# A recommendation tower on one core: first table looked up by high and low parts, TensorE run beforehand on the identity, and another order of units, turns and grams for the first tiles

## The reference

```python
e = stack([tbl_f[ids[:, f]] for f in range(26)], axis=1)       # 2048 x 26 x 128
combined = concatenate([e, r_dense_x[:, None, :]], axis=1)     # 2048 x 27 x 128
z = einsum('bfd,bgd->bfg', combined, combined)[:, triu_i, triu_j]
h = concatenate([z, r_dense_x], axis=1)                        # 2048 x 479
h = maximum(h @ W_top1 + b_top1, 0)                            # 512
h = maximum(h @ W_top2 + b_top2, 0)                            # 256
y = h @ W_top3
```

## Time and profile before

| | us |
|---|---|
| median of 3 runs | 369.84 |
| the three runs | 369.84, 367.74, 370.93 |
| profiled execution, first to last instruction | 368.7 |

### The profile page before, as it was taken

The page is one execution under the profiler, slowest core; times in us unless marked ns, Lnnn a source line. Parts: engine busy times, 40 slices in busy tenths (PEclk is TensorE's granted clock), DMA queues, the critical chain, the costliest instruction groups (busy, mean ns, idle before and its releaser), DMA issues.

```text
span 368.7 us, 12553 instructions
## 1 busy us (share of the span) xinstructions
PE 339.9 (92%) x5616; PEld 282.4 (77%) x5616; DVE 170.0 (46%) x388; ACT 187.5 (51%) x260; POOL 259.5 (70%) x265
## 2 busy tenths in 40 slices
PE   1999889698999999999999999999999999889677
PEld 0488877586888888887888788888888888877576
DVE  3599955555254635356255535356255534202020
ACT  2399831553636734583627634483627633564313
POOL 6788877777777777777777777777777777776000
PEclk9999999999999999999999999999999999999989
DMA  6969394244243333423242334424232222222000
GB/s 231 338 198 245 95 281 129 54 114 94 58 118 80 81 94 100 103 71 112 66 110 80 89 87 100 106 70 110 65 111 80 66 52 73 54 53 72 3 4 1
DMA packets 19369, 37.33 MB, mean 101 GB/s; under 512 B 5525, under 2 KB 8213, under 8 KB 19316
## 3 DMA queue, kind: packets, MB, share of 16 engines
q1 hardware_dynamic: 11124, 19.74, 18.6%
q0 software_dynamic: 8192, 16.79, 17.4%
HBM read 36.51 MB, written 0.01 MB: 99 GB/s over the span
## 4 chain that ended last, share of the span: by engine, by line
POOL 57%; issue 20%; PE 13%; DVE 5%; DMA 3%; ACT 2%; POOLq 0%; SPq 0%
POOL rows L263 57%; DVE onehot L298 3%; PE ps_lk L552 3%; PE ps_lk L576 2%; PE ps_gram L602 2%; DMA h<-in_tbl 2%; PE ps_lk L657 2%; DVE table L304 1%; DMA rows<-in_tbl,gather_ids 1%; PE ps_lk L672 1%; PE ps_mlp L636 1%; PE ps_zt L629 1%; ACT xt L374 0%; PE ps_zt L636 0%; PE ps_mlp L629 0%
## 5 line engine op out<-in xcount | busy, mean ns | idle before, releaser
L263 POOL DMA_INDIRECT rows<-in_tbl,gather_ids x256 | 258.2, 1009 | 79.7 <-issue 77.1
L298 DVE TENSOR_SCALAR onehot<-ids 128x512 fp32r<-128x512 f32 (+1 forms) x328 | 126.8, 442 | 84.0 <-PE ps_lk L576 51.2
L576 PE MATMUL ps_lk<-onehot,table 128*128 128x512 f32 (+1 forms) x704 | 155.3, 374 | 4.5 <-DVE onehot L298 3.4
L576 PEld LDWEIGHTS ps_lk<-onehot,table 128*128 128x128 f32 x704 | 120.5, 190 | 25.7 <-issue 5.3
L384 ACT COPY xt<-ps_tr 128x512 f32<-128x512 f32 x64 | 76.8, 1200 | 73.9 <-PE ps_tr L587 73.9
L312 DVE STREAM_TRANSPOSE zs<-ps_gram 128x832 f32<-128x832 f32 x16 | 16.8, 1050 | 99.9 <-PE ps_gram L602 99.9
L602 PEld LDWEIGHTS ps_gram<-xt 128*26 128x26 f32 x4096 | 44.0, 104 | 23.3 <-issue 20.3
L602 PE MATMUL ps_gram<-xt 128*26 128x26 f32 x4096 | 53.0, 193 | 9.2 <-issue 4.8
L371 ACT COPY xt<-ps_lk 128x512 f32<-128x512 f32 x35 | 42.0, 1235 | 21.6 <-issue 9.6
L587 PE MATMUL ps_tr<-ident,rows 128*128 128x128 f32 x256 | 39.4, 276 | 2.6 <-DMA rows<-in_tbl,gather_ids 2.3
L587 PEld LDWEIGHTS ps_tr<-ident,rows 128*128 128x128 f32 x256 | 29.9, 140 | 9.5 <-issue 4.0
(11 more groups left out here) (59 smaller groups left out, 157.6 us busy)
## 6 DMA issues: line engine op xcount, KB each, us to landing
ids<-in_ids_onehot SPq DMA_DIRECT2D x41, 256.0 KB
rows<-in_tbl,gather_ids POOLq DMA_INDIRECT x256
w<-in_tbl SPq DMA_DIRECT2D x6, 512.0 KB, 6.7
zt<-in_tbl SPq DMA_DIRECT2D x3, 512.0 KB, 7.0
dense_x<-in_dense SPq DMA_DIRECT2D x8, 128.0 KB
zt<-in_dense SPq DMA_DIRECT2D x8, 128.0 KB, 2.7
h<-in_tbl SPq DMA_DIRECT2D x1, 512.0 KB, 6.1
w<-in_w SPq DMA_DIRECT2D x1, 512.0 KB
```

The costliest lines, as they stand in the source:

```text
L263: pool.indirect_dma_start(rows[n % ROW_BUFS][:, r, :], None, t_[f"tbl_{GATHERED[r]}"], bass.IndirectOffsetOnAxis(ap=gather_ids[:, n, r:r + ...
L298: nc.vector.tensor_scalar(onehot[:, k, 0:w], ids[e % IDS][:, 0:w].bitcast(F32), float(k), None, ALU.is_equal).then_inc(s_unit, 1)
L576: m = nc.tensor.matmul(ps_lk[e % LB][:, x], table[:, i, part, k, :], onehot[:, k, x], start=(k == 0 and j == 0 and part == 0), stop=(k == ...
```

## The change

Five things change.

1. Step 0 is looked up like the others, from the high and low parts. Table 0 is split first, in two halves of four k each (`FIRST_PARTS`), ScalarE and VectorE each with two operations of half the size. `lookup(0)` waits for each half. `split_count(j)` is the number of splitting operations after which table j is ready, since table 0 now counts two.
2. Staging: all five buffers are used in turn by all ten tables.
3. TensorE multiplies the identity with itself 20 times into an unused PSUM bank ahead of the first lookup (`WARM_UP`).
4. VectorE makes the units of the fourth step of chunk 1 ahead of pack(1), and in the middle of the units of step 0 the two halves of table 0 are subtracted. ScalarE's order of rounding, shifting ids and copying is altered to suit in the first steps.
5. TensorE's turns, lookups and grams of tiles 0 to 2 are in another order.

```diff
-SPLIT = list(range(1, NO)) + [0]
+FIRST_PARTS = 2
+WARM_UP = 20
...
-        RAWS = len(stage) - 1
-        raw = [stage[0] if j == 0 else stage[1 + SPLIT.index(j) % RAWS] for j in range(NO)]
+        RAWS = len(stage)
+        raw = [stage[j % RAWS] for j in range(NO)]
...
+        def split_count(j):
+            return FIRST_PARTS + j
...
-                n = SPLIT.index(j)
-                if j > 0 and n >= RAWS:
-                    sp.wait_ge(s_low, n - RAWS + 1)
+                if j >= RAWS:
+                    sp.wait_ge(s_low, split_count(j - RAWS))
...
-            sp.wait_ge(s_low, NO)
+            sp.wait_ge(s_low, split_count(NO - 1))
...
+            def low_first(part):
+                k = slice(part * KT // FIRST_PARTS, (part + 1) * KT // FIRST_PARTS)
+                dve.wait_ge(s_high, part + 1)
+                nc.vector.tensor_tensor(table[:, 0, 1, k, :], raw[0][:, k, :],
+                                        table[:, 0, 0, k, :].bitcast(F32), ALU.subtract).then_inc(s_low, 1)
...
-            make_units(0)
+            make_units(0, range(0, 4))
+            low_first(0)
+            make_units(0, range(4, 6))
+            low_first(1)
+            make_units(0, range(6, KT))
             for e in range(1, STEP0[1]):
...
-            low(NO - 1)
...
+            def high_first(part):
+                k = slice(part * KT // FIRST_PARTS, (part + 1) * KT // FIRST_PARTS)
+                act.wait_ge(s_raw[0], 16)
+                nc.scalar.copy(table[:, 0, 0, k, :], raw[0][:, k, :]).then_inc(s_high, 1)
...
-            def lookup_first():
-                pe.wait_ge(s_raw[0], 16)
-                for k in range(KT):
-                    pe.wait_ge(s_unit, k + 1)
-                    m = nc.tensor.matmul(ps_lk[0][:, :], raw[0][:, k, :], onehot[:, k, :].bitcast(F32),
-                                         start=(k == 0), stop=(k == KT - 1))
-                    if k % USE == USE - 1:
-                        m.then_inc(s_unit_used, 1)
+            def warm_up():
+                for _ in range(WARM_UP):
+                    nc.tensor.matmul(ps_zt[:, 0:P], ident[:, :], ident[:, :], start=True, stop=True)
...
+                    if e == 0 and k % (KT // FIRST_PARTS) == 0:
+                        pe.wait_ge(s_low, k // (KT // FIRST_PARTS) + 1)
...
-            lookup_first()
+            warm_up()
+            lookup(0)
```

More of the change, by code:

```diff
@@ L291, in _, with make_units @@
         def _(dve):
-            def make_units(e):
-                dve.wait_ge(s_from, e + 1)
-                for k in range(KT):
+            def make_units(e, ks=range(KT)):
+                if ks[0] == 0:
+                    dve.wait_ge(s_from, e + 1)
+                for k in ks:
                     if k % USE == 0 and e > 0:
@@ L325, in _ @@
             nc.vector.tensor_copy(first[:, :], first_i[:, :]).then_inc(s_first, 1)
-            make_units(0)
+            make_units(0, range(0, 4))
[3 more added lines that the diff above has]
+            make_units(0, range(6, KT))
             for e in range(1, STEP0[1]):
-                for n in range(len(STEPS[e][2])):
-                    low(STEPS[e][2][n] - 1)
+                for j in STEPS[e][2]:
+                    low(j)
                 make_units(e)
-            low(NO - 1)
             dve.wait_ge(s_const, 3)
@@ L353, in _, with high @@
         def _(act):
-            def high(n):
-                j = SPLIT[n]
+            def high_first(part):
+                k = slice(part * KT // FIRST_PARTS, (part + 1) * KT // FIRST_PARTS)
+                act.wait_ge(s_raw[0], 16)
+                nc.scalar.copy(table[:, 0, 0, k, :], raw[0][:, k, :]).then_inc(s_high, 1)
+            def high(j):
                 act.wait_ge(s_raw[j], 16)
@@ L422, in _ @@
             shift(0)
-            high(0)
+            high_first(0)
+            high_first(1)
+            high(1)
             shift(1)
-            high(1)
+            high(2)
+            shift(2)
             evac(0)
-            shift(2)
             evac_group(0, 0)
-            high(2)
+            high(3)
             shift(3)
             evac(1)
-            high(3)
+            high(4)
             shift(4)
@@ L435, in _ @@
             evac_group(0, 1)
-            high(4)
             high(5)
@@ L443, in _ @@
             evac(4)
+            evac_group(0, 3)
             high(7)
-            evac_group(0, 3)
+            high(8)
             shift(7)
             evac(5)
-            high(8)
+            evac(6)
             high(9)
+            evac_group(1, 0)
             shift(8)
-            evac(6)
-            evac_group(1, 0)
             evac_dense(0)
@@ L699, in _ @@
             e = STEP0[1]
+            turn(1, 1)
             gram(0, 0)
-            turn(1, 1)
             lookup(e)
@@ L704, in _ @@
             gram(0, 1)
+            lookup(e + 1)
             turn(1, 3)
-            lookup(e + 1)
+            lookup(e + 2)
             gram(1, 0)
-            lookup(e + 2)
+            turn_pairs(0)
             gram(1, 1)
@@ L713, in _ @@
                 a, e, f = c * CT, STEP0[c], STEP0[c + 1]
-                turn_pairs(a - 2)
+                if c > 1:
+                    turn_pairs(a - 2)
                 if c == 1:
@@ L731, in _ @@
                     turn(a, 3)
-                gram(a, 0)
-                lookup(f)
+                    lookup(f)
+                    gram(a, 0)
+                else:
+                    gram(a, 0)
+                    lookup(f)
                 turn(a + 1, 0)
```

14 lines of the change are left out of this document (5 added, 9 removed).

## The result

The changed kernel takes 367.54 us, the median of 14 runs (364.89 to 422.55), the kernel before 370.42 in the 14 runs beside it (367.74 to 371.54). The ratio is 0.9924, with a 95% interval of 0.9899 to 0.9949: 2.8 us faster, between 1.9 and 3.7. The profiled execution of the changed kernel took 366.06 us on the device for a span of 363.6. The difference, some 2.4 in the changed kernel's runs, is 1.7 in those of the kernel before, so 0.7 us of what the spans gain is given back outside them.

The account below looks back on a forecast made before the run. The prediction took GpSimd's back-to-back gathers, the last one's landing and a fixed tail as the bound. The ninth gather's stall (0.82 us) plus less stretching (0.6) made 1.4 us off the median of 369.84: 368.4, range 365.8 to 370.9.

Parts of the forecast that it names:

- within 1%: Whole kernel: the measured time lies within 1% (3.7 us) of the time before; given 0.82.
- Term one: Ninth gather, waiting for k = 3 of the first lookup: its stall goes, 0.82 us gained.
- Term two: Gathers stretched by VectorE's subtractions: somewhat fewer caught than before, 0.6 us gained.
- TensorE is some 8 us ahead at 80 us: TensorE's early part: a lead of 3.7 us and 4 us, plus the wait at turn(1, 3).
- A distance so constant ... is a wait for the rows: Tiles 6 to 12: turn(n, 3) starts 4.01 to 4.14 us after its gather, so TensorE waits for rows to land.
- the 4.0 it must have: turn(3, 3): it must start 4.0 us after its gather; at 8.45 it had 4.4 us of room.
- What it gains early it waits away: TensorE, faster than the gathers by some 0.4 us a round, loses any early lead in waits for rows.
- A fixed tail: From turn(15, 1) to the end: the last 36.5 us are TensorE's and ScalarE's own and stay.
- Rival A: Whole kernel: TensorE is the bound, so its lead of 8.2 us survives whole, 361.6 us; 8%.
- B: First 42 us: VectorE, packed tighter, stretches gathers more, 3.1 us lost against 0.82 gained, 372.1 us; 12%.
- C: New waits at turn(3, 3) and turn(4, 3) let the clock fall, costing 1.6 us if late, 370.0 us; 10%.
- D: Lookup 0: the warm-up ends late and the clock is low, most of the ninth gather's stall stays, 369.2 us; 5%.

Follow-up runs that it names:

- experiment 1: Changed kernel with ScalarE's rounding of table 9 moved ahead of the copy of lookup 6, two sets: 367.12 us (0.9929) and 368.02 us (0.9961).
- reorder alone: Kernel before with only the new order of VectorE's units and TensorE's turns, lookups and grams: 370.68 us, ratio 1.0000.
- experiment 2: One gather fewer a tile from tile 2 on: on the changed kernel 362.39 us, on that with table 9's rounding moved 361.59, on the kernel before 366.16.
- experiment 3: Changed kernel with GpSimd's gathers held once ahead of tile 3, until four units of lookup 11 are used: 370.06 us, ratio 1.0006.
- experiment 5: Changed kernel with the warm-up removed: 369.92 us, ratio 0.9982.
- lookup alone: Changed kernel with the old order of tiles 0 to 2 on TensorE and VectorE, two sets: 372.15 us (0.9969) and 370.54 us (0.9992).

## Why the prediction was right, and where it was wrong

The number came out: 367.54 for 368.4, within the range, and "within 1%" was the case that held. But the gain was 2.8 where 1.4 was forecast, and its reason covers only a part; that the rest stayed within the range is luck, since no term had it. The account in spans: at turn(15, 3) the two changed profiles are 2.2 and 1.5 us early, the tail is 2.9 shorter, and 0.7 is lost outside the span: 4.4 and 3.6, against 2.8 and 3.5 by the two ratios.

- Term one, the stall of the ninth gather: right that it goes. But the gather starts at 14.44 for the 14.07 of the forecast, 0.45 earlier than before and not 0.82, in the first profile. The second lookup (13.32 for 13.8) and the warm-up (8.02, within 6.0 to 10.3) are near where they were put.
- Term two, less stretching: right in the sum for the first profile (1.61 by the last gather for 1.4), most of it from here: the seventeenth gather is only 0.11 earlier than before, the thirty-third 1.50. But the second profile of the same kernel has the last gather 1.74 earlier still, so single gathers stretch differently from one execution to the next, and a term of 0.6 was below what one profile can carry.
- "TensorE is some 8 us ahead at 80 us": wrong. At turn(2, 3), near 84 us, it was 0.16 behind in the first profile and 2.9 ahead in the second, at turn(3, 3) 1.2 ahead in both. The sum followed VectorE's work alone and left out ScalarE's new order, whose rounding of table 9 came 3.85 us late for VectorE; and the lookup near 70 us, which was to lose its wait and run at the upper level, took 6.78 us.
- "A distance so constant ... is a wait for the rows": the conclusion holds for the kernel before, the argument does not. Before, the last packet of the rows ended 0.41 to 0.58 us ahead of the turns of tiles 6 to 12, as at turns held by name (0.31 to 0.94 in four profiles), and these turns start 0.20 to 0.31 us behind the start of the matmul ahead of them, 0.11 in the changed kernel. So they were held, but by 0.1 to 0.2 us each, some 1.1 in all with turn(15, 1). After the change the distance is as constant, 5.17 to 5.18, with the rows there 2.98 to 3.01 us ahead.
- Such constancy is not chance either: in the eleven profiles with all gathers, 41 of the 44 distances at these tiles lie within 3.9 to 4.3, 5.1 to 5.3, 6.4 to 6.5, 7.7 to 7.8 or 8.9 to 9.0, one gather step of 1.25 apart. Something couples the two streams, mostly without a wait of either; VectorE, which waits for TensorE and stretches gathers, could, but no run isolates it. And "the 4.0 it must have" fell: turns held by name measured 2.70 to 4.22 from tile 4 on.
- "What it gains early it waits away": half right. An earlier TensorE gained nothing (experiment 1, reorder alone), but hardly more where fewer gathers could not hold it (experiment 2); later gathers cost time (experiment 3). And a later TensorE costs time as well (experiment 5, lookup alone). The streams look balanced within a microsecond or two, and that the change pays because it moves both is argued from these runs, not shown.
- "A fixed tail": wrong, and the largest error in size. The 36.5 us from turn(15, 1) became 33.4.
- Rival A (TensorE bound, 361.6) had the bound that the page after shows, but not the 8 us. B did not come: the last gather is not later. C did come, at 42 and 70 us and not at the waits for rows. D did not.

The runs sorted by their mean granted clock show no shift of the bound (means in us, with the count of runs; those of the kernel before are from the experiments):

| clock | before | changed |
|---|---|---|
| 0.994 to 0.995 | 366.6 (3) | 364.9 (4) |
| 0.990 to 0.991 | 369.5 (40) | 365.9 (7) |
| 0.985 to 0.986 | 370.0 (19) | 368.0 (11) |
| 0.981 to 0.982 | 370.5 (28) | 366.1 (1) |

From the first row to the third both kernels lose about as much, 3.4 and 3.1 us. At like clock the changed one is faster in every row, by 1.7 to 3.6 where both have more than one run.

## What to carry to other kernels

A constant distance between two streams shows a wait only if the row names it or a later producer moves it; look when the rows land, and whether the turn starts later behind the matmul ahead of it than elsewhere. Where two streams are as long as each other, undo each part of a change alone: here no part shows a gain and all together do. And compare the stretches that the change does not touch, the tail above all, since moving or adding instructions anywhere ahead can move pauses there.

## What was not expected of the hardware

- Pauses of TensorE within runs of small matmuls, for which the profile names no releaser: 0.8 to 2.4 us in the tail, 4.1 to 4.2 at 91 us. The Trainium skill (Runtime: NRT & Kernel Launch, section "Instruction fetch mechanics") says that an engine's program is refilled in 16 KiB blocks and that the cost of crossing a block is mostly hidden. The packets are of that size; that the cost is hidden these traces do not bear out, if the 42 pauses that end 2.2 to 2.9 us after a packet begins are the crossings.
- The tail's 2.2 to 2.4 us pause had the lower clock behind it in all three profiles that have it, which cost another 1.4 us of matmul time in the kernel before; the tail's pauses up to 1.16 us had none. In grams at 88 to 115 us pauses of 1.51, 1.64, 1.68 and 1.84 us had it behind them, in four profiles, and one of 1.77, in one of these profiles, had not: length alone does not decide it.
- Gathers begun inside a two-input subtraction took 1.90 us again (18.69), where 0.94 is the undisturbed one. In the three profiles of the two kernels all 18 gathers that begin 0.1 to 0.9 us into a subtraction end 0.81 or 0.82 us after it ends, wherever in it they began: it looks as if the gather's work waits for the subtraction. The Trainium skill (SBUF — State Buffer, section "Who interferes with whom") infers that a two-input operation does not hold up descriptors; these rows do not agree. It also says that on this chip an operation with at most one input in SBUF, outside the modes that use both ports, does not contend with GpSimd, and a fill has none; yet a gather begun 0.10 us ahead of a fill took 2.11. Whether the fill or the units behind it did that was not isolated.
